# Gated cross-attention and expert layer: key blocks added in pairs on GpSimd ahead of the ones product, and a reordered seam

## What is computed

```python
x = x + tanh(g_xattn) * xattn(layernorm(x), ctx, ctx, Wq, bq, Wk, bk, Wv, bv, Wo, bo)
#   attn = softmax(Q K^T / sqrt(32)) over the keys; out = attn V; out @ Wo.T + bo
x = x + tanh(g_ffn) * ffn(layernorm(x), Wr, br, W1, b1, W2, b2)
#   8 experts, top 2 of a softmax router, capacity 615 tokens each;
#   h = silu(xg @ W1 + b1); out = h @ W2 + b2; times the gate, added back by token
```

## Time and profile before

| | |
|---|---|
| median of 3 runs | 1820.79 us (1820.72 to 1822.04) |
| profiled execution | 1820.35 us, span 1818.6 us |
| PE busy | 1722.9 us, 95% |
| DVE busy | 1077.2 us, 59% |
| ACT busy | 798.5 us, 44% |
| POOL busy | 435.4 us, 24% |
| mean granted PE clock | 0.975 of full speed |

### The profile page before, as it was taken

One profiled execution on the slowest core, in us unless ns is written; L12 is line 12 of the kernel. 1 busy time (PEld: TensorE's weight loads), 2 busy tenths in 40 slices (PEclk: granted clock), 3 DMA queues, 4 the chain that ended last, 5 costly groups with the idle time before them and its releaser, 6 DMA issues.

```text
span 1818.6 us, 29436 instructions
## 1 busy us (share of the span) xinstructions
PE 1722.9 (95%) x10322; PEld 828.1 (46%) x10322; DVE 1077.2 (59%) x2087; ACT 798.5 (44%) x1092; POOL 435.4 (24%) x424
## 2 busy tenths in 40 slices
PE   7999999999999999999716999999999999999998
PEld 4324243342423334242304647465665747565563
DVE  6777867778776777867587625345352625434231
ACT  4563735546364554735322516153342616244240
POOL 2332434223333332421211121211121121112101
PEclk9999999999999999999956999999999999999999
DMA  6334263433425433343122553635253362626312
GB/s 225 106 77 132 72 164 114 103 121 98 140 93 143 134 93 116 90 112 99 47 94 82 140 138 100 161 86 158 73 163 90 105 160 86 177 49 177 77 45 28
DMA packets 214606, 203.17 MB, mean 112 GB/s; under 512 B 121812, under 2 KB 162912, under 8 KB 210456
## 3 DMA queue, kind: packets, MB, share of 16 engines
q1 hardware_dynamic: 193432, 181.80, 33.0%
q0 software_dynamic: 21120, 20.67, 6.4%
HBM read 134.57 MB, written 43.63 MB: 98 GB/s over the span
## 4 chain that ended last, share of the span: by engine, by line
PE 84%; DVE 9%; issue 3%; ACT 2%; POOL 1%; DMA 1%; SPq 0%; DVEq 0%; ACTq 0%; POOLq 0%
PE psum L1556 23%; PE psum L1532 21%; PE psum L1354 7%; PE psum L1361 6%; PE psum L1345 6%; PE psum L1335 6%; PE psum L1325 6%; PE psum L1447 4%; PE psum L1372 3%; DVE mx L925 2%; DVE reached L1077 1%; DVE x2hl L997 1%; DVE x2hl L999 1%; DVE stats L877 1%; DVE x2n L884 1%
## 5 line engine op out<-in xcount | busy, mean ns | idle before, releaser
L1556 PE MATMUL psum<-w,hT 128*128 128x512 f16 (+1 forms) x1920 | 415.7, 379 | 0.0
L1532 PE MATMUL psum<-xgT,w 128*128 128x308 f16 (+1 forms) x3072 | 409.7, 294 | 0.8 <-DVE xgT L1178 0.8
L925 DVE TENSOR_REDUCE mx<-psum 128x1 f32<-128x512 f32 x512 | 330.1, 683 | 105.6 <-PE psum L1335 104.0
L1532 PEld LDWEIGHTS psum<-xgT,w 128*128 128x128 f16 x3072 | 296.8, 97 | 110.2 <-DVE xgT L1178 1.1
L779 ACT ACTIVATE pt<-psum 128x1024 f32<-128x1024 f32 x256 | 255.1, 1022 | 116.3 <-PE psum L1345 116.3
L1556 PEld LDWEIGHTS psum<-w,hT 128*128 128x128 f16 (+1 forms) x1920 | 199.3, 104 | 213.8
L851 ACT ACTIVATE h<-psum,b1c 128x308 f32<-128x308 f32 (+1 forms) x256 | 118.1, 512 | 343.3 <-PE psum L1532 342.9
L1199 DVE TENSOR_TENSOR hT<-h,hT 128x615 f16<-128x615 f32 x128 | 102.5, 801 | 211.5 <-ACT hT L854 211.5
L672 POOL DMA_INDIRECT out_dram<-y,idx_now x40 | 88.0, 2201 | 498.4 <-DVE y L1231 311.7
L1228 DVE SCALAR_TENSOR_TENSOR y<-psum,b2b 128x512 f32<-128x512 f32 (+1 forms) x40 | 27.7, 692 | 270.1 <-PE psum L1556 270.1
L1325 PE MATMUL psum<-actT,wT 128*128 128x512 f16 x768 | 179.2, 381 | 2.0 <-DVE wT L912 2.0
(11 more groups left out here) (187 smaller groups left out, 1511.8 us busy)
## 6 DMA issues: line engine op xcount, KB each, us to landing
stage<-in_L_ffn_W_dram SPq DMA_DIRECT2D x62, 1024.0 KB, 5.8
stk<-qk_rows SPq DMA_DIRECT2D x192, 128.0 KB, 2.5
qk_rows<-qks SPq DMA_DIRECT2D x64, 256.0 KB, 2.5
xin<-in_x_dram SPq DMA_DIRECT2D x8, 1024.0 KB, 5.4
cin<-in_ctx_dram SPq DMA_DIRECT2D x8, 1024.0 KB, 7.6
xres<-in_x_dram SPq DMA_DIRECT2D x8, 1024.0 KB, 5.6
out_dram<-xres SPq DMA_DIRECT2D x32, 256.0 KB, 2.1
x_split<-x2hl SPq DMA_DIRECT2D x32, 256.0 KB, 2.3
```

The costliest lines, as they stand in the source:

```text
L925: v.reduce_max(mx[:, KT * t + qt:KT * t + qt + 1], ps, AX.X).then_inc(read, 1)
L1532: mm = t_.matmul(psum[:, (2 * m + ch) % 4, 0:c1 - c0], w1[:, wp, kt, m * P:(m + 1) * P], xgT[:, KT * xp + kt, c0:c1], start=(kt == 0 and ( ...
L1556: mm = t_.matmul(psum[0:rows, Y_BANK[i], :], hT[:, hp, k, c * P:c * P + rows], w2[:, wp, k, :], start=(k == 0 and (hp, wp) == (0, 0)), sto ...
```

## The change

- `with_ones` no longer runs once a unit. For units 0 to 7 POOL adds unit 2p + 1 to unit 2p in place (four adds of 128 x 512 float32), and PE multiplies the sum with ones once; units 8 to 15 keep a product each. `SUMS` fixes the slots. PE waits on `pair_added`; ACT, before it overwrites a unit's buffer, on `sums_done`. There are now five buffers for units: `pt` has two, and `qk32`, `x2nT` and `x2n` lend the others.
- PE's order in a slot becomes S0, S1, filling, less_maxima 0, ones, S2, less_maxima 1, S3, values.
- The reciprocals become a transpose of 32 x 32 blocks, a reciprocal of 16 columns, and a transposed broadcast. Norm slots move to 16, 18, 20, 23; ACT's split one slot later.
- The next x is normalised on DVE in slots 5 and 6 in place of POOL.
- `STORE_GROUP` is 0: the row stores and the load of `xres` stand behind group 0, slot 4. POOL's bias adds wait for the load alone and stand ahead of the pairs.
- After the last batch, tiles are normalised, turned and multiplied one by one, and two by two, with matmuls in between whose result is not used (`keep_clock`).
- Only SP waits for the last stores. The first expert's W2 loads wait for the five gathers. PE runs unused matmuls (`keep_busy`) before and between the transposes of the gathered chunks.

```diff
-STORE_GROUP = 1
+STORE_GROUP = 0
 GROUP_END = [LAG_C + 4 * g + 3 for g in range(NG)]
-RECIP_SLOT = ((11, 12, 13, 14), (15, 16, 16, 17), (19, 19, 20, 20), (23, 23, 23, 23))
-GROUP_NORM = [slots[-1] for slots in RECIP_SLOT]
+PAIRS, PT_UNITS = 4, 5
+SUMS = {10: (("pair", 0),), 12: (("pair", 1),), 14: (("pair", 2),), 16: (("pair", 3),), 17: (("unit", 8),),
+        18: (("unit", 9), ("unit", 10)), 19: (("unit", 11),), 20: (("unit", 12), ("unit", 13)),
+        21: (("unit", 14),), 22: (("unit", 15),)}
+SUM_ORDER = [term for slot in sorted(SUMS) for term in SUMS[slot]]
+SUM_COUNT = len(SUM_ORDER)
+GROUP_SUMS = [[i for i, (kind, n) in enumerate(SUM_ORDER) if n // (2 if kind == "pair" else 4) == g] for g in range(NG)]
+SUMS_END = [max(slot for slot in SUMS for term in SUMS[slot] if SUM_ORDER.index(term) in GROUP_SUMS[g]) for g in range(NG)]
+GROUP_NORM = [16, 18, 20, 23]
+GROUP_SPLIT = [17, 19, 21, 23]
+X_NORM_SLOT = (5, 5, 6, 6)
...
+
+def sum_of_unit(u):
+
+    return SUM_ORDER.index(("pair", u // 2) if u < 2 * PAIRS else ("unit", u))
...
         pt = sb("pt", [P, 4, 2, S], f32)
+        pt_units = ([pt[:, 2 * i:2 * i + 2, :, :] for i in range(2)]
+                    + [a.rearrange("p (a b) s -> p a b s", b=2) for a in (qk32[:, :, :], x2nT[:, :, :], x2n[:, :, :])])
...
...
             def expert(e, last):
 
+                if isinstance(e, int) and e == 0:
+                    for c in range(C):
+                        sp.wait_ge(xg_first[c], 16)
                 for i in range(4):
                     chunk(8 * e + 4 + i, i, W2[e, i * 4 * P:(i + 1) * 4 * P, :], 4)
...
                     if i == QK_FIRST + 2:
+                        if not last:
+                            for tt in range(KT - 1):
+                                inverse_deviation(0, tt, KT * b + (KT + tt))
                         pool.wait_ge(mrow_ready, NG * b + 1)
+                    if i == QK_FIRST + 3 and not last:
+                        inverse_deviation(0, KT - 1, KT * b + (2 * KT - 1))
                     pool.wait_ge(qk32_ready, NQ * b + i + 1)
...
                     g.tensor_tensor(qks[:, n, 1, m, :], qk32[:, i % 4, :], qks[:, n, 0, m, :],
                                     ALU.subtract).then_inc(qk_split, 1)
-                pool.wait_ge(mrow_ready, NG * b + 2)
-                if not last:
-                    for tt in range(KT):
-                        n = KT * b + (KT + tt)
-                        inverse_deviation(0, tt, n)
-                        pool.wait_ge(ln_rstd[0], n + 1)
-                        settle(pool)
-                        g.tensor_scalar(xn[:, tt, :], xin[:, tt, :], mv[:, 0, tt, 0:1], rstd[:, 0, tt:tt + 1],
-                                        ALU.subtract, ALU.mult).then_inc(xn_ready, 1)
-
-                pool.wait_ge(mrow_ready, NG * b + 3)
                 pool.wait_ge(xres_in, 16 * b + 16)
                 pool.wait_ge(tgbo_ready, 1)
                 for tt in range(KT):
                     g.tensor_tensor(xres[:, tt, :], xres[:, tt, :], tgbo[:, :], ALU.add).then_inc(xres_biased, 1)
+                for p in range(PAIRS):
+
+                    if p % 2 == 0:
+                        pool.wait_ge(mrow_ready, NG * b + (p // 2 + 2))
+                    pool.wait_ge(pv_done, UNITS * b + (2 * p + 1))
+                    for hf in range(2):
+                        copied(pool, use, ("ST", 2 * p + 1, hf), b)
+                        for j in range(2):
+                            into = pt_units[2 * p % PT_UNITS][:, hf, j, :]
+                            g.tensor_tensor(into, into, pt_units[(2 * p + 1) % PT_UNITS][:, hf, j, :],
+                                            ALU.add).then_inc(pair_added, 1)
+
...
-                            act.wait_ge(pv_done, UNITS * b + max(u - 1, 0))
+                            if u < PT_UNITS:
+                                act.wait_ge(sums_done, SUM_COUNT * b)
+                                act.wait_ge(qk_split, NQ * b + NQ)
+                            else:
+                                act.wait_ge(sums_done, SUM_COUNT * b + (sum_of_unit(u - PT_UNITS) + 1))
                             bank, _ = use(("ST", u, hf), b)
                             _, read = filled(act, use, ("ST", u, hf), b)
-                            s.activation(pt[:, (2 * u + hf) % 4, :, :], psum[:, bank:bank + 2, :], ACT.Exp,
+                            s.activation(pt_units[u % PT_UNITS][:, hf, :, :], psum[:, bank:bank + 2, :], ACT.Exp,
...
+                    if t in SUMS_END[:-1]:
+                        gr = SUMS_END.index(t)
+                        act.wait_ge(sums_done, SUM_COUNT * b + (GROUP_SUMS[gr][-1] + 1))
+                        act.wait_ge(norm_done, NG * b + max(gr - 1, 0))
                         s.activation(osum[:, gr % 2, 1, :], psum[:, 7, :], ACT.Copy).then_inc(sums_ready, 1)
...
-            rows, sums, logits = router_copy(post, 0, B)
-            rows()
-            sums()
-            logits()
+            for tt in range(KT):
+                ps, read = filled(act, post, ("x2T", tt))
+                s.activation(x2nT[:, :, tt * P:(tt + 1) * P], ps.rearrange("p (k q) -> p k q", q=P), ACT.Copy).then_inc(read, 1)
+            for part, (t0, t1) in enumerate(LAST_PARTS):
+                ps, read = filled(act, post, ("lg_parts", part))
+                s.activation(lg_parts[:, t0 * P:t1 * P], ps[:, 0:(t1 - t0) * P], ACT.Copy).then_inc(read, 1)
+            ps, read = filled(act, post, "lg")
+            s.activation(lg[:, B, :], ps[:, 0:KT * E], ACT.Copy).then_inc(read, 1)
...
-                def reciprocals(g, quarters):
+                def inverse_sums(g):
                     if g < NG - 1:
-                        dve.wait_ge(osum_ready, (NG - 1) * b + g + 1)
                         dve.wait_ge(sums_ready, (NG - 1) * b + g + 1)
                         sums = osum[:, g % 2, 1, :]
                     else:
 
-                        dve.wait_ge(pv_done, UNITS * b + UNITS)
+                        dve.wait_ge(sums_done, SUM_COUNT * b + SUM_COUNT)
                         dve.wait_ge(norm_done, NG * b + g)
                         sums = psum[:, 7, :]
-                    for i in quarters:
-                        v.reciprocal(osum[:, g % 2, 1, i * P:(i + 1) * P], sums[:, i * P:(i + 1) * P]).then_inc(rinv_done, 1)
+                    v.transpose(turned_sums[:, :], sums).then_inc(sums_turned, 1)
+                    dve.wait_ge(sums_turned, NG * b + g + 1)
+                    own = mx[:, NT // 2 * g:NT // 2 * g + NT // 2]
+                    v.reciprocal(own, turned_sums[:, :].rearrange("p (c k) -> p c k", k=32)[:, :, 0:1].rearrange(
+                        "p c k -> p (c k)")).then_inc(sums_inverted, 1)
+                    dve.wait_ge(sums_inverted, NG * b + g + 1)
+                    v.transpose(osum[:, g % 2, 1, :].rearrange("p (c k) -> p c k", k=32),
+                                own.rearrange("p (c o) -> p c o", o=1).to_broadcast((P, NT // 2, 32))).then_inc(rinv_done, 1)
...
-                        for quarter in range(4):
-                            if t == RECIP_SLOT[g][quarter]:
-                                reciprocals(g, (quarter,))
+                        if t == GROUP_NORM[g]:
+                            inverse_sums(g)
                     if t in GROUP_NORM:
                         g = GROUP_NORM.index(t)
-                        dve.wait_ge(rinv_done, KT * (NG * b + g + 1))
+                        dve.wait_ge(rinv_done, NG * b + g + 1)
+                        if g < NG - 1:
+                            dve.wait_ge(osum_ready, (NG - 1) * b + g + 1)
 
                         dve.wait_ge(a_hi, NG * b + g)
                         dve.wait_ge(a32_ready, NG * b + g)
                         v.tensor_tensor(t32[:, :], osum[:, g % 2, 0, :] if g < NG - 1 else psum[:, 6, :], osum[:, g % 2, 1, :],
                                         ALU.mult).then_inc(norm_done, 1)
                     if not last:
+                        for tt in range(KT):
+                            if t == X_NORM_SLOT[tt]:
+                                normalise(0, tt, KT * b + (KT + tt), xin[:, tt, :], xn[:, tt, :], xn_ready)
...
-                for tt in range(KT):
+                    if last and tt == KT - 2:
+                        normalise(1, 0, KT * b, xres[:, 0, :], x2n[:, 0, :], x2n_ready)
+                for tt in range(1 if last else 0, KT):
                     normalise(1, tt, KT * b + tt, xres[:, tt, :], x2n[:, tt, :], x2n_ready)
...
-                            t_.matmul(psum[32 * j:32 * j + 32, 6, :], v32[:, kt, HD * h:HD * h + HD],
-                                      pt[:, (2 * u + j // 2) % 4, j % 2, :], start=(kt == 0), stop=(kt == KT - 1))
-
-                def with_ones(u):
-                    if 0 <= u < UNITS:
-                        kt = u % 4
+                            last = t_.matmul(psum[32 * j:32 * j + 32, 6, :], v32[:, kt, HD * h:HD * h + HD],
```

(98 more changed lines are left out.)

## The result

The changed kernel takes 1881.99 us (median of 4 runs, 1880.84 to 1883.56), the kernel before 1820.76 beside it: ratio 1.0339, 95% interval 1.0323 to 1.0356. The forecast was 1880 us.

What follows compares the result with a forecast made beforehand. PE's instruction list was taken to bound the kernel: 1820.35 + 66 (attention, mainly stalls on pair 0) - 6.5 (seam) = 1880 us, 3.3% slower. The range takes in 1855 and 1905; the forecast was given 0.7.

Steps and rivals of the forecast that it cites:

- The cause: Slot 10: PE waits for pair 0, behind the xres load and bias adds on GpSimd; 10.3 us a loop batch.
- the frame of before: Times of batch 2 in the earlier kernel's trace, where slot 7 starts at 289.25; batches 1 to 7 repeat it.
- PE's stall: PE's wait for pair 0 in slot 10: 10.3 us in each of seven batches, 4.9 in batch 0.
- PE's list: PE's instructions with nothing late, 12 ones products for 16: -3.0 us a batch, -24 us for eight.
- short slot: Score slot without a ones product, including a 0.33 us stall: 3.15 us against 3.93, six a batch, -4.7 us together.
- The late slots: Slots 16 to 22, with 9 ones products where there were 7: +1.7 us a batch.
- The later pairs: Pairs 1 to 3 ready before PE asks; the margin at pair 2 is only 0.7 us.
- The clock: PE's first 3.3 us behind each stall run at half rate: +1.65 us a batch, bounds 0 and 3.3.
- The seam: From last batch to experts: -3.7 at the logits, -2.0 at the fifth gather, -0.8 clock; -6.5 us, bounds -9 and -2.
- The sum: Whole kernel: 1820.35 + 66 - 6.5 = 1880 us, 3.3% slower.
- attention: All eight batches: seven at +8.95 us and batch 0 at +3.5, +66 us.
- rival 1: Pair 0 in time at 299.7, slot 10: 1790 us, chance 0.1; the turn to faster at xres landed by about 294.2.

Runs made afterwards that it cites:

- first experiment: Changed kernel with GpSimd's wait for xres and its bias adds moved from ahead of pair 0 to between pairs 1 and 2: 1797.01 us, ratio 0.9876.
- second: Changed kernel with STORE_GROUP back at 1, so row stores and the xres load stand in slot 8 again: 1947.03 us in one run.
- the last: Changed kernel with STORE_GROUP = 1 and the bias adds behind all four pairs: 1788.28 us, ratio 0.9823.

## Why the prediction was right

- **The cause** was named with its place: pair 0, in slot 10, behind the load and the bias adds. The trace of after shows it, and moving the one block (first experiment) or shifting the load (second) moves the time as the chain says.
- **The chain, step by step, in the frame of before** (subtract 12.16): last stacking predicted 288.77, seen 288.89; load issued 294.3, seen 294.4; landed 299.9, bias adds start at 300.7; pair 0 ready 309.9, seen 310.5; the ones product at 310.0, seen 310.5. The add was priced by the earlier trace rows at 4.96 us for four and took 4.92. The estimate from the GPSIMD Engine Reference of the Trainium skill, 4.5 us, was too low; the row decided rightly. The page also says that GpSimd and VectorE contend for SBUF when a VectorE instruction has two SBUF inputs (or runs in a 2-port perf mode). The traces agree as far as they go: four adds took 4.92 us with DVE idle in the changed kernel's stall, and 4.96 beside the maxima, which read PSUM, in the first experiment.
- **PE's stall**: 7 x 10.3 + 4.9 = 77 us predicted; 68.1 for GpSimd and 9.2 for the maxima's transfers, 77.3, seen. I had written that those transfers land within the stall at 299.5; they land later, behind the stores and the load (PE gets them at 312.93 - 12.16 = 300.8), and only stayed hidden because pair 0 was later still. The first experiment uncovered them, 7.1 us, and in the last 1.7 us of such waits are left. That the stall came out right all the same was luck: for PE it makes no difference which of the two it waits for.
- **PE's list**: a short slot of 3.15 us predicted, 3.17 seen. The late slots, 366.19 - 345.78 = 20.4 us, are 1.3 longer than before, not 1.7: the two products more cost 1.7 as predicted, but slot 19 lost the wait for ACT's copy (2.82 us against 3.18), which the prediction did not count.
- **The later pairs** stayed hidden. Pair 2 was ready at 339.08 and asked for at 339.66, 0.6 us later, where I had 0.7.
- **The clock** was undersized. I took a recovery 3.3 us after PE starts again in each batch, from the two places in the earlier trace rows; the windows behind the eight stalls show 3.1 to 6.3 us, 36.5 in all, and filling the stall gave back 18 us where I had counted 13.
- **The seam**: -6.5 predicted, -8.0 seen. The first router step came 22.15 us after the start of the last output products, before 25.80 (908.94 - 883.14): -3.7 at the logits as predicted. Up to the expert it is -2.9 (I had -2.0), and the whole of the clock's gain, 1.4, where I took half.
- **The sum**: attention came to +68.5 where I had +66. With 77.3 us of waits and 18 of clock, PE's list must have gained 27 us, 3.4 a batch, where I had 24. The price of the clock was put 5 us too low, the gains of the list and of the seam 3 and 1.5 us. The errors have opposite signs, so that the forecast is within 2 us is in part luck; the sign and the size of the loss are not.
- **The turn of rival 1** was worked out wrong. By the prediction's own terms, stall and lost clock (10.3 + 1.65) must shrink by 7.6 us to reach 4.35, so xres would have had to land by 292.3, not 294.2. The rival was farther off than it says.

## What to carry to other kernels

When work is handed to a side engine, its time per item may be the smaller question, as it was here; find what stands ahead of the first item in that engine's list, and the latest transfer that this waits for. Here 5 us of bias adds that nobody needed until the batch's end, tied to a late load, stood ahead of work that PE needed in slot 10; moved behind the first two pairs the same adds turned 3.4% slower into 1.2% faster, and behind all pairs, with the load back in its old place, into 1.8% faster. No run tried the other way, a later slot on PE for the product of pair 0. And a wait of 5 to 9 us on PE, as here, costs more than its length, since the products behind it run at half rate.

## What the runs showed of the hardware

- The granted clock came back 3.1, 3.4, 3.8, 4.0, 4.5, 5.3, 5.9 and 6.3 us after PE resumed, behind eight stalls of 5 to 9.4 us in one execution. The price of a fall is then a spread of 1.5 to 3.2 us, not one number. "TensorE: Matmul & The Clock Gate" of the Trainium skill (HAM oscillation) describes the same pattern for waits on DMA, a fall and a new ramp in every step; here it is a wait on GpSimd, and it cost 18 us.
- Fillers placed in a stall of known length (40 matmuls of 128 x 512, 8.7 us) held the clock in this kernel: in batch 2 it is 1.00 in every window of two us from 308 to 322, and the mean over the span is 0.981 with them and 0.958 without.
- With two banks for four scores and one reader, spacing decides: the same instructions in another order made slots of 3.15 us into slots of 3.58, and batches of 106.1 us into ones of 107.2, though no engine had more to do.
